# A decoder layer with routed experts on one core: the two expert sums loaded one behind the other, and part of the closing sum moved to GpSimd

## The reference

```python
x = layernorm(x + self_attention(x))          # one head, 256 wide, bias in and out
x = layernorm(x + cross_attention(x, ctx))    # 16 heads, 64 keys, padding mask and causal mask
x = layernorm(x + experts(x))                 # 16 experts, the 4 best of each token

def layernorm(x, eps=1e-05):
    m, v = mean(x, -1), var(x, -1)
    return (x - m) / sqrt(v + eps)

# experts: probs = softmax(x @ router_w + router_b), 4 largest, scaled to sum 1
# out = sum over chosen experts e of  share_e * (gelu(x @ w1[e] + b1[e]) @ w2[e] + b2[e])
```

## Time and profile before

| what | value |
|---|---|
| three executions | 619.87 us median, 618.16 to 623.65 |
| the profiled execution, its own time | 620.94 us |
| its span, first to last instruction | 618.9 us |
| last matmul ends | about 587 us |
| last scatter issued, landed | 590.57 us, 594.31 us |
| first load of the sums issued | 594.40 us |
| first and last addition on DVE begin | 597.95 us, 611.35 us |
| mean granted TensorE clock | 0.931 |

### The profile page before, as it was taken

One profiled execution on the slowest core, in us unless ns is written; L12 is line 12 of the kernel. 1 busy time (PEld: TensorE's weight loads), 2 busy tenths in 40 slices (PEclk: granted clock), 3 DMA queues, 4 the chain that ended last, 5 costly groups with the idle time before them and its releaser, 6 DMA issues.

```text
span 618.9 us, 14447 instructions
## 1 busy us (share of the span) xinstructions
PE 542.2 (88%) x4060; PEld 510.0 (82%) x4060; DVE 426.8 (69%) x1061; ACT 343.6 (56%) x627; POOL 289.1 (47%) x262
## 2 busy tenths in 40 slices
PE   6999999999789989898398999999999999999700
PEld 5978888888678988787267999999999999999700
DVE  2646655555567878786555878888878888888436
ACT  2433333333245656564223877878777878787504
POOL 5641111111111456566550256776676767676633
PEclk9999999999989999996555999999999999999965
DMA  8899999600000112122259699999999999999377
GB/s 276 300 397 397 398 396 398 232 0 0 1 1 2 47 68 78 69 75 82 91 173 307 181 272 262 249 265 255 258 255 266 250 254 253 261 257 236 44 186 247
DMA packets 91675, 124.37 MB, mean 201 GB/s; under 512 B 6624, under 2 KB 62832, under 8 KB 91648
## 3 DMA queue, kind: packets, MB, share of 16 engines
q1 hardware_dynamic: 73984, 102.31, 50.1%
q0 software_dynamic: 14592, 19.41, 15.7%
q10 hardware_dynamic: 3072, 2.33, 1.2%
HBM read 61.88 MB, written 62.14 MB: 200 GB/s over the span
## 4 chain that ended last, share of the span: by engine, by line
PE 74%; DVE 7%; issue 7%; DMA 4%; ACT 3%; POOL 2%; another core or an unknown queue 1%; SPq 0%; DVEq 0%; ACTq 0%; POOLq 0%
PE ps L348 19%; PE ps L350 18%; PE ps L349 18%; PE ps L908 3%; PE ps L891 2%; PE ps L736 2%; PE ps L809 2%; PE ps L799 2%; DMA expert_rows<-xd,idx 2%; POOL expert_rows L551 2%; PE ps L825 1%; PE ps L770 1%; PE ps L791 1%; DMA x_all<-in_x 1%
## 5 line engine op out<-in xcount | busy, mean ns | idle before, releaser
L570 POOL DMA_INDIRECT expert_sum<-yb,home_row x80 | 166.5, 2081 | 105.6 <-DVE home_row L1491 85.3
L348 PE MATMUL ps<-gT_h,w_h 128*128 128x256 f32 x320 | 94.7, 296 | 1.8 <-issue 1.3
L348 PE MATMUL ps<-w_h,h_h 128*128 128x256 f32 x320 | 90.8, 284 | 1.9 <-DVE h_l L1484 1.9
L349 PE MATMUL ps<-gT_l,w_h 128*128 128x256 f32 x320 | 91.4, 286 | 0.0
L350 PE MATMUL ps<-gT_h,w_l 128*128 128x256 f32 x320 | 91.4, 286 | 0.0
L350 PE MATMUL ps<-w_h,h_l 128*128 128x256 f32 x320 | 90.6, 283 | 0.0
L349 PE MATMUL ps<-w_l,h_h 128*128 128x256 f32 x320 | 90.6, 283 | 0.0
L551 POOL DMA_INDIRECT expert_rows<-xd,idx x64 | 62.8, 981 | 33.8 <-issue 22.9
L1484 DVE TENSOR_TENSOR h_l<-hf,h_h 128x1024 fp32r<-128x1024 f32 x40 | 49.0, 1225 | 39.9 <-ACT h_h L1108 38.0
L1101 ACT ACTIVATE hf<-ps,b1s 128x256 f32<-128x256 f32 x160 | 62.8, 478 | 24.7 <-PE ps L350 24.4
L348 PEld LDWEIGHTS ps<-gT_h,w_h 128*128 128x128 f32 x320 | 62.2, 194 | 2.4 <-issue 1.5
(11 more groups left out here) (239 smaller groups left out, 1373.1 us busy)
## 6 DMA issues: line engine op xcount, KB each, us to landing
expert_rows<-zeros SPq DMA_DIRECT2D x32, 1088.0 KB, 13.6
w1f<-in_L_ffn_w SPq DMA_DIRECT2D x40, 512.0 KB
w2f<-in_L_ffn_w SPq DMA_DIRECT2D x40, 512.0 KB
xg<-expert_rows SPq DMA_DIRECT2D x40, 272.0 KB
total<-expert_sum SPq DMA_DIRECT2D x16, 256.0 KB, 5.6
expert_sum<-zeros SPq DMA_DIRECT2D x1, 2304.0 KB, 15.9
x_all<-in_x SPq DMA_DIRECT2D x8, 256.0 KB, 7.2
expert_sum<-x_all ACTq DMA_DIRECT2D x8, 256.0 KB
```

The source lines that it names most:

```text
L348: pe.matmul(o, ah, bh, start=first, stop=False)
L349: pe.matmul(o, ah, bl, start=False, stop=False)
L570: pool.indirect_dma_start(out=sums[p], out_offset=bass.IndirectOffsetOnAxis(ap=home_row[:, p, c:c + 1], axis=0), in_=yb[:, p, c], in_offse ...
```

## The change

SP now loads the even sum as soon as its own two kinds of scatter (`st_y[0][0]` and `st_y[0][1]`) have landed, with 4 DMAs of 512 KB that all count on a new semaphore `even_in`. Then it waits for the odd scatters and loads the odd sum alone, with 8 DMAs of 256 KB on `pair_in[m]`. An addition waits for the whole even sum and for the odd sum of its own pair. Two of the eight additions, those of pairs 2 and 5, are done on GpSimd: pair 2 ahead of the root of pair 0, pair 5 ahead of the root of pair 3. Epsilon is added on GpSimd too, for every pair, in the new function `root3`, directly ahead of the power and with a wait between the two. DVE's instruction for it is gone, and DVE's wait for the root of the pair before the last one now stands ahead of `bn_aggr`. The `passed` increments are fillers between waits.

```diff
+EVEN_LOAD = 2
+POOL_ADDS = (2, 5)
...
-            for p in range(2):
+            for p, (half, landed, size) in enumerate(((total, lambda m: even_in, EVEN_LOAD), (total2, lambda m: pair_in[m], 1))):
                 for c in range(2):
                     sp.wait_ge(st_y[p][c], more * 16 + 16 * PAIRS_LEAST)
-            for m in range(NT // 2):
-                for p, half in enumerate((total, total2)):
-                    sp.dma_start(half[:, 2 * m:2 * m + 2], sums[p][m * 2 * P:(m + 1) * 2 * P, :].rearrange("(a p) d -> p a d", p=P)).then_inc(pair_in[m], 16)
+                sp.sem_inc(passed, 1)
+                for m in range(0, NT // 2, size):
+                    sp.dma_start(half[:, 2 * m:2 * (m + size)], sums[p][m * 2 * P:(m + size) * 2 * P, :].rearrange("(a p) d -> p a d", p=P)).then_inc(landed(m), 16)
...
-            for m in range(NT // 2):
-                pool.wait_ge(evar, m + 1)
+            def root3(m):
+                pool.wait_ge(ebna, 2 * m + 2)
                 if m >= 2:
                     pool.wait_ge(eo, 2 * m - 2)
+                pool.tensor_scalar(tve[:, m % 2], tmv[:, m % 2, :, 1], EPS, 0.0, ALU.add, ALU.add).then_inc(evar, 1)
+                pool.wait_ge(evar, m + 1)
                 pool.tensor_tensor(trstd[:, m % 2], tve[:, m % 2], mhalf[:].broadcast_to([P, 2]), ALU.pow).then_inc(erst, 1)
+
+            def add_pair(m):
+                pool.wait_ge(even_in, 16 * (NT // 2 // EVEN_LOAD))
+                pool.wait_ge(pair_in[m], 32)
+                pool.tensor_tensor(total[:, 2 * m:2 * m + 2], total[:, 2 * m:2 * m + 2], total2[:, 2 * m:2 * m + 2], ALU.add).then_inc(gtot, 1)
+
+            for m in range(NT // 2):
+                if m + 2 in POOL_ADDS:
+                    add_pair(m + 2)
+                root3(m)
...
+            own = [m for m in range(NT // 2) if m not in POOL_ADDS]
             for m in range(NT // 2):
-                dve.wait_ge(pair_in[m], 48)
-                dve.tensor_tensor(total[:, 2 * m:2 * m + 2], total[:, 2 * m:2 * m + 2], total2[:, 2 * m:2 * m + 2], ALU.add).then_inc(etot, 1)
-                dve.wait_ge(etot, m + 1)
+                if m in POOL_ADDS:
+                    dve.wait_ge(gtot, POOL_ADDS.index(m) + 1)
+                else:
+                    dve.wait_ge(even_in, 16 * (NT // 2 // EVEN_LOAD))
+                    dve.wait_ge(pair_in[m], 32)
+                    dve.tensor_tensor(total[:, 2 * m:2 * m + 2], total[:, 2 * m:2 * m + 2], total2[:, 2 * m:2 * m + 2], ALU.add).then_inc(etot, 1)
+                    dve.wait_ge(etot, own.index(m) + 1)
                 for a in range(2):
                     dve.bn_stats(tbn[:, m % 2, a], total[:, 2 * m + a]).then_inc(ebns, 1)
                 dve.wait_ge(ebns, 2 * m + 2)
                 if m >= 2:
                     dve.wait_ge(shift_ok, m - 1)
+                    dve.wait_ge(erst, m - 1)
                 for a in range(2):
                     dve.bn_aggr(tmv[:, m % 2, a], tbn[:, m % 2, a]).then_inc(ebna, 1)
                 if m >= 1:
                     shifts(m - 1)
-                dve.wait_ge(ebna, 2 * m + 2)
-                if m >= 2:
-                    dve.wait_ge(erst, m - 1)
-                dve.tensor_scalar(tve[:, m % 2], tmv[:, m % 2, :, 1], EPS, None, ALU.add).then_inc(evar, 1)
             shifts(NT // 2 - 1)
```

More of the change, by code:

```diff
@@ L342, in decoder_layer @@
         pair_in = [sem(f"pair_in{m}") for m in range(NT // 2)]
-        etot = sem("etot"); ebns = sem("ebns"); ebna = sem("ebna"); evar = sem("evar"); erst = sem("erst"); shift_ok = sem("shift_ok"); eo = sem("eo")
+        even_in = sem("even_in")
+        gtot = sem("gtot"); etot = sem("etot"); ebns = sem("ebns"); ebna = sem("ebna"); evar = sem("evar"); erst = sem("erst"); shift_ok = sem("shift_ok"); eo = sem("eo")
         st_o = sem("st_o")
```

## The result

The changed kernel takes 623.66 us in the median of 20 runs (620.13 to 629.03), the kernel before 619.12 in 20 runs beside them. The two medians lie 4.5 us apart; the measured ratio is 1.0064, with a 95% interval of 1.0041 to 1.0086, and this makes 4.0 us slower, from 2.5 to 5.3. The forecast was 2.1 us slower, 622.0, with a range of 617.7 to 625.1. The loss is smaller than the 1% that the forecast took for what can be told from no change, but with 20 runs of each kernel no change lies outside the interval. The changed kernel's profiled span is 621.9 us against 618.9.

The account below looks back on a forecast made before the run. The prediction took DVE to bound the end stretch, with the loads running ahead. Its terms, +2.2 - 0.8 - 1.4 + 2.1 = +2.1 us, added to the median 619.87 gave 622.0 us, range 617.7 to 625.1.

Parts of the forecast that it names:

- DVE's start: First addition, after the whole even sum and first odd piece: at 600.5 instead of the equivalent of 598.27, +2.2 us.
- epsilon off DVE: Epsilon instruction gone from DVE's step for each pair: about 0.1 us saved eight times, -0.8 us.
- two additions off DVE: Additions of pairs 2 and 5 moved to GpSimd: 0.72 us each with the step behind, -1.4 us.
- DVE and the roots held up: DVE waits at pairs 1 and 4 while GpSimd adds pairs 2 and 5: 1.0 and 1.1 us, +2.1 us.
- slow beginning: Start of the load stream: 286 GB/s in the first 4.3 us, 357 afterwards; 2 MB in 7.5 us, 6.0 without it.
- just covered: First odd load after a late scatter landing, 597.6 + 2.8 = 600.4: still hidden by the queue of even loads.
- The hold at the port: Two-operand SBUF instructions of DVE and GpSimd exclude each other; DVE waits 1.0 and 1.1 us beside GpSimd's additions.
- No hold: Rival, chance 0.25: DVE and GpSimd add side by side, +0.6 us in sum, 620.5.
- The loads come early: Rival, chance 0.17: even stream at its later rate throughout, DVE starts at 598.7, port not held; -1.2 us, 618.7.
- POOL becomes the bound: Rival, chance 0.13: GpSimd's chain aggregate, epsilon, power, shift binds, +1.2; with the scatter counted in full +4.2 us, 624.1.

Follow-up runs that it names:

- even_first_late: The changed kernel, but SP waits for all scatters before the first load, then loads the even sum and then the odd one; ratio 1.0054.
- early_only: The kernel before with only the early load of the even sum; all additions and epsilon stay on DVE; ratio 1.0039.
- adds_write_only: The changed kernel with the two additions on GpSimd replaced by two memsets each, so pairs 2 and 5 are not summed; ratio 1.0009.
- no_pool_adds: The changed kernel with all eight additions back on DVE; early even load and epsilon on GpSimd stay; ratio 1.0039.
- even_behind_odd0: The changed kernel, but SP waits for three of the four scatters before it loads the even sum; ratio 1.0059.
- late_two_eps: The kernel before with epsilon on GpSimd and the even halves of pairs 0 and 1 loaded once three of four scatters landed; ratio 0.9990.
- eps_only: The kernel before with epsilon on GpSimd alone, additions and loads as before, run twice; ratios 1.0020 and 0.9980.
- adds_only: The kernel before with only the additions of pairs 2 and 5 on GpSimd, loads and epsilon as before; ratio 1.0029.

## Why the prediction came out as it did

The direction held, and so did the sign of every sum in the table. The loss was larger than forecast, 3.4 against 2.1 us in the traces, and one term makes nearly all of the difference. The right column goes by the first trace of the kernel before; by the second one, whose pair 1 landed 0.6 us later, the start is +2.7 and the sum +2.8, so how much of the miss is real and how much is that landing stays open by 0.6 us.

| term | forecast | in the traces |
|---|---|---|
| DVE's start | +2.2 | +3.3 |
| epsilon off DVE | -0.8 | -1.0 |
| two additions off DVE | -1.4 | not seen alone |
| DVE and the roots held up | +2.1 | not seen alone |
| both together | +0.7 | +1.1 |
| sum | +2.1 | +3.4 |

**The start was mis-sized.** I put the even sum's end at 599.7, 9.1 us behind the scatter; it came at 10.1, a little above my upper bound (600.6, 10.0). From the first even issue it is 10.2 us in the changed kernel and 8.6 in even_first_late, where no scatter is beside the loads. So the term that was too small is the scatters' share in the even stream: 1.6 us, where I had added 0.3 from a span of 0 to 1.2 for the last scatter alone. Then come 0.75 us for the first odd quarter megabyte, as in the forecast. The rest of the stream, 1.4 + 7.5 = 8.9 us, was right within 0.3, but not for my reason: even_first_late lands its 512 KB loads 1.5 us apart from the first on (8.1, 9.6, 11.1, 12.6). There the 8.6 us hold a fixed part of the landing and no slow beginning.

**The cover was thinner than "just covered".** The forecast let the scatter land 3.7 to 6.9 us behind its issue. In the four kernels that issue the whole even sum ahead of it (the changed one, early_only, adds_write_only, no_pool_adds) it landed at 7.5, 7.8, 7.8 and 8.8. An odd load issued at once then lands some 2.7 or 2.8 us later, and the queue of even loads lets it land 0.75 us behind the even sum. In the changed kernel the issue alone would give 7.6 + 2.8 = 10.4 and the queue 10.1 + 0.75 = 10.9, and it landed at 10.9: the queue decided, by half a microsecond. In early_only and adds_write_only the two meet at 10.6. In no_pool_adds the lateness reached DVE, 0.8 us. The even loads were issued 0.05, 0.14, 0.10 and 0.30 us ahead of the scatter in these four kernels, so the later landings go with the longer lead; four traces don't show that it is the cause.

**Why is the scatter late?** Look at the queues from 2 us behind it on, when its packets flowed before. The kernel before, 592.57 to 594.57:

```profile
DMA packets 144, 0.13 MB, mean 66 GB/s; under 512 B 16, under 2 KB 144, under 8 KB 144
## 3 DMA queue, kind: packets, MB, share of 16 engines
q0 software_dynamic: 144, 0.13, 59.7%
```

The changed kernel, 592.15 to 594.95:

```profile
DMA packets 728, 0.73 MB, mean 260 GB/s; under 512 B 16, under 2 KB 728, under 8 KB 728
## 3 DMA queue, kind: packets, MB, share of 16 engines
q1 hardware_dynamic: 728, 0.73, 86.0%
```

And the changed kernel from 595.05 to 597.75:

```profile
q1 hardware_dynamic: 731, 0.73, 79.7%
q0 software_dynamic: 144, 0.13, 30.9%
```

q0 carries the scatters, q1 SP's loads. Most of the delay isn't a stretching by sharing: for 2.8 us not one of the scatter's 144 packets moves, and then they pass in 2.2 us (595.1 to 597.3) instead of 1.3 (592.7 to 594.0). The Trainium skill (DMA: Bandwidth & Descriptors, "Queues, rings and completion order") has each DMA engine take turns between its queues, a packet at a time, and its packet is a bundle of descriptors, typically 9 to 17 and at most 64. The profile counts smaller things: of a scatter's 144 packets 128 are its rows of 1 KB. The last window agrees with the turns, 144 packets of q0 among 731 of q1. The window before it does not show a turn for q0 at all, while q1's 728 are about 45 for each of the 16 engines: several bundles of the typical size, though not yet one of the largest. What fits all runs, and is no more than a summary of them, is that loads queued before the scatter's packets start hold them back, by 0.2 us for 256 KB, 1.6 for 512 KB and 3.8 to 5.0 for 2 MB, and loads queued later don't (even_behind_odd0, late_two_eps). What it is that waits, the fetch of the scatter's descriptors or the packets, the traces don't tell; this stays open.

**The hold at the port was right, in both orders.** I had the rows for one order only: GpSimd's power waiting for DVE's addition, 1.06 against 0.69 us. The other order now shows as 1.70 against 0.69 and 1.12 against 0.13 us, 1.0 us each, as the forecast had it (1.0 and 1.1). The rule of the Trainium skill (SBUF — State Buffer, "Who interferes with whom") thus holds here, and so does its other half, that a GpSimd instruction which only writes does not contend: 0.13 and 0.69 across the memsets. Two things were off. The second time the shift was caught, since it has two SBUF inputs as well. And DVE's steps for pairs 2 and 5, without an addition of their own, take 1.26 and 1.25 us instead of 1.05, because each ends with a wait for the root of the pair before. These two waits are the 0.4 us by which the two together miss.

**The rivals.** "No hold" is out by those two durations. "The loads come early" is out: DVE began at 11.0 us, not at 8.1. "POOL becomes the bound" is out where it was placed: epsilon takes 0.22 us alone and 0.56 to 0.73 beside an addition of DVE, which hides the difference, and DVE's pairs stay at 1.72 us. GpSimd's chain does bind in the two steps without an addition, for 0.2 us each. The measured +4.0 us lies nearer to this rival's +4.2 than to my +2.1, but of its terms only the late start came true, not the +1.2. SP's early issue at 590.10 shows that the change does what it says.

## What to carry to other kernels

An early load is worth only what the first consumer gains: here it moved half of the data forward, while the first step needed all of that half and then a piece of the other, so 4 us of earlier issue turned into a start 3.3 us later. Before giving VectorE's additions to GpSimd, look at which of VectorE's instructions beside them read two SBUF operands, down to the smallest: GpSimd's additions of 1.26 us took 1.0 us each from VectorE, for 0.72 saved. And a load put ahead of a scatter that others wait for can hold it up by more than the scatter takes.

## What the runs showed that I had not expected

- A scatter on the software queue stood still for 2.8 us beside 2 MB of loads whose issue began 0.05 us before its own, while the DMA engines moved the loads at 260 GB/s, and 2 MB queued 2.1 us after its issue did not touch it (3.8 us). But those loads themselves then took 1.1 us longer than with no scatter under way.
- The first odd load landed 2.8 us behind its issue on an idle queue, 3.3 behind the even sum in the changed kernel, and 4.5 us in late_two_eps with only 512 KB ahead of it.
- Pair 1 of the interleaved loads landed 9.6, 10.1, 10.2, 10.5 and 10.5 us behind the scatter in five executions with the same loads (the kernel before and eps_only twice, adds_only once). That microsecond is as large as everything that epsilon's move gains.
